# Expert rows transposed on their way in by DMA, as two planes of 16-bit halves, with the picks for four blocks taken together

## The reference, cut to what matters

```python
x = x + 0.5 * ffn(layernorm(x), ...)      # 32 experts, 6 per token, and shared experts
x = x + attn(layernorm(x), ...)           # local in segments of 64, global over 64 means
x = x + 0.5 * ffn(layernorm(x), ...)      # the same weights again
# in ffn, for every expert e that a token chose, with weight c:
g = xf @ gu[:128].T ; u = xf @ gu[128:].T
routed += c * (silu(g) * u @ dn.T)
```

## Time and profile before

| | us |
|---|---|
| median of three runs | 1511.45 (1508.77 to 1520.38) |
| profiled execution, its span | 1514.0 |
| first load of expert rows to last issue of answers, first expert stage (L515, L672) | 272.1 to about 630 |
| the same, second expert stage | 1049.9 to 1407.8 |
| PE busy | 1311.2 (87%) |
| DVE busy | 1092.3 (72%) |
| POOL busy | 921.6 (61%) |
| ACT busy | 745.8 (49%) |

### The profile page before, as it was taken

One profiled execution on the slowest core, in us unless ns is written; L12 is line 12 of the kernel. 1 busy time (PEld: TensorE's weight loads), 2 busy tenths in 40 slices (PEclk: granted clock), 3 DMA queues, 4 the chain that ended last, 5 costly groups with the idle time before them and its releaser, 6 DMA issues.

```text
span 1514.0 us, 50415 instructions
## 1 busy us (share of the span) xinstructions
PE 1311.2 (87%) x10768; PEld 1150.5 (76%) x10769; DVE 1092.3 (72%) x5484; ACT 745.8 (49%) x2296; POOL 921.6 (61%) x981
## 2 busy tenths in 40 slices
PE   6877772799999999789989998952999999999986
PEld 5766661699999999678766766742999999999765
DVE  6676654478888888576368888863788888888576
ACT  3433320466666666300356666721666666666100
POOL 3777777466666666422017776775566666666687
PEclk9776775899999999899699999955999999999998
DMA  9963333465556555397003333444565556564698
GB/s 316 404 248 130 126 130 127 146 184 184 186 185 190 181 187 178 119 330 256 1 29 136 142 131 131 147 174 144 176 188 187 184 183 186 180 184 139 231 315 280
DMA packets 155771, 275.35 MB, mean 182 GB/s; under 512 B 28966, under 2 KB 108091, under 8 KB 155712
## 3 DMA queue, kind: packets, MB, share of 16 engines
q1 hardware_dynamic: 115776, 161.32, 34.6%
q0 software_dynamic: 39936, 113.33, 20.2%
HBM read 147.64 MB, written 135.27 MB: 187 GB/s over the span
## 4 chain that ended last, share of the span: by engine, by line
PE 30%; DVE 7%; DMA 5%; issue 4%; POOL 3%; ACT 1%; DVEq 0%; SPq 0%; POOLq 0%; ACTq 0%
PE ps L711 26%; DMA ans<-answers 4%; PE ps L831 3%; POOL dispatch_rows L656 2%; DVE smax L1926 1%; DVE yb L1846 1%; POOL xres L693 1%; DVE stats L1469 0%; DVE prob L1936 0%; DVE rstd L1456 0%; DVE newt L1454 0%; DVE newt L1455 0%; PE ps L719 0%; DMA blk<-normed_transposed 0%; POOL answers L672 0%
## 5 line engine op out<-in xcount | busy, mean ns | idle before, releaser
L711 PE MATMUL ps<-xbt,ans 128*128 128x128 f32 x3584 | 477.0, 276 | 0.3 <-ACT ans L1274 0.3
L711 PEld LDWEIGHTS ps<-xbt,ans 128*128 128x128 f32 x3584 | 439.0, 193 | 0.9 <-ACT ans L1274 0.8
L672 POOL DMA_INDIRECT answers<-yb,didx x224 | 220.2, 983 | 160.9 <-issue 118.0
L672 POOL DMA_INDIRECT answers<-ans,didx x224 | 220.1, 983 | 122.2 <-issue 120.2
L1703 DVE SCALAR_TENSOR_TENSOR picked<-iota_e,etab,blk 128x32 f32<-128x32 f32 x896 | 190.7, 250 | 119.9 <-DVE yb L1724 40.1
L656 POOL DMA_INDIRECT dispatch_rows<-blk,idx x192 | 188.4, 981 | 142.9 <-issue 129.3
L1274 ACT COPY ans<-wgu 128x512 f32 x448 | 274.6, 613 | 0.2 <-issue 0.2
L711 PE MATMUL ps<-wdn,hb 128*128 x896 | 267.6, 381 | 1.3 <-DVE ans L1724 1.3
L632 POOL DMA_INDIRECT dispatch_rows<-blk,idx x192 | 187.3, 976 | 79.0 <-issue 57.2
L1280 ACT ACTIVATE sg<-ps 128x128 f32<-128x128 f32 x448 | 124.4, 278 | 218.5 <-PE ps L711 216.8
L831 PE MATMUL ps<-ident,blk 128*128 128x128 f32 x896 | 172.9, 275 | 33.6 <-DMA blk<-dispatch_rows 33.6
(11 more groups left out here) (230 smaller groups left out, 1996.7 us busy)
## 6 DMA issues: line engine op xcount, KB each, us to landing
blk<-dispatch_rows SPq DMA_DIRECT2D x448, 160.0 KB
ans<-answers SPq DMA_DIRECT2D x54, 512.0 KB, 4.9
ans<-answers SPq DMA_DIRECT2D x54, 256.0 KB, 4.8
wgu<-in_gate_up SPq DMA_DIRECT2D x32, 256.0 KB
dispatch_rows<-blk,idx POOLq DMA_INDIRECT x384, 2.5
dispatch_rows<-padt SPq DMA_DIRECT2D x32, 160.0 KB
yb<-answers SPq DMA_DIRECT2D x10, 512.0 KB, 4.8
wdn<-in_down SPq DMA_DIRECT2D x16, 256.0 KB
```

The lines of the kernel that those rows point to most:

```text
L672: pool.indirect_dma_start(out=answers_dram, out_offset=bass.IndirectOffsetOnAxis(ap=didx[:, q:q + 1], axis=0), in_=block_answers(q), in_of ...
L711: return nc.tensor.matmul(out_, lhs, rhs, start=start, stop=stop)
```

## The change: what it does

**The rows.** A row in `dispatch_rows` keeps its 1,280 bytes and is laid out as two planes of 640 bytes. Plane 0 holds 256 16-bit halves (the one half of each float) and the 32 weights. Plane 1 holds the other halves and the 32 destinations. ACT's copy in `act_route_rows` writes the planes: it moves 2 x 2 x 256 elements of 16 bits per partition in place of 512 floats. The scatters of the routing name the same bytes as 16-bit elements.

**The loads.** SP issues two DMAs per block in place of one. A transposing DMA takes 256 source rows (128 rows x 2 planes) of 256 16-bit elements and writes them transposed, so that the two halves of each float lie side by side again: 128 partitions x 2 x 128 floats. There are eight such buffers. A second DMA loads the weights and destinations, 2 runs of 128 bytes per row, into one of two buffers, each for four blocks. The register with the first row number is read one block ahead, by `reg_load`, without the range check.

**What goes.** PE's two transpositions per block, ACT's copy of them, and their semaphores go.

**The picks.** DVE compares the expert number for four blocks at once (`mark`), multiplies with the loaded pairs (`take`), reduces (`reduce_`) and makes four indices (`lists`), one of these per step: four instructions for four blocks in place of 20 records. PE's down product has four PSUM banks in place of two.

```diff
-COL_W, COL_DEST = D, D + E
+PLANE = ROW // 2
+COL_W, COL_DEST = D // 2, PLANE + D // 2
...
-        LOADS, ANSWERS = 4, 8
+        LOADS, ANSWERS, PICKED, LISTS = 8, 8, 4, 16
...
-            def body(g, peeled):
-                for q in range(LOADS):
-                    n = g * LOADS + q
-                    first = sp.value_load(itab[0:1, bass.ds(n + 2 * P, 1)], min_val=0, max_val=E * CAP - P)
-
-                    if not peeled:
-                        sp.wait_ge(s.tx, n - (LOADS - 1))
-                        sp.wait_ge(s.pick, n * 2 - (2 * LOADS - 2))
-                    sp.dma_start(block_rows(q), rows_dram[bass.ds(first, P), :]).then_inc(s.ld[q], 16)
...
+            def load(n, q, m=None):
+                at_ = sp.snap(first[q % 2], min_val=0, max_val=E * CAP - P)
+                if m is None or n + 1 < NB:
+                    sp.reg_load(first[1 - q % 2], itab[0:1, bass.ds(n + 1 + 2 * P, 1)])
+                block_rows = rows_dram[bass.ds(at_, P), :]
+
+                positive(sp, s.gu, n - (LOADS - 1))
+                sp.dma_start_transpose(
+                    out=turned_halves(q % LOADS),
+                    in_=block_rows.bitcast(U16).rearrange("r (h x) -> (r h) x", h=2)[:, 0:D]
+                    ).then_inc(s.ld[q % LOADS], 16)
+
+                positive(sp, s.pick, n // PICKED - 1 if isinstance(n, int) else turn_of(n, q) - 1)
+                sp.dma_start(pairs_of(q // PICKED % 2)[:, q % PICKED],
+                             block_rows.rearrange("r (h x) -> r h x", h=2)[:, :, D // 2:]
+                             ).then_inc(s.pairs[q // PICKED % 2], 16)
...
-            def tx(n, q):
-
-                b = q % LOADS
-                pe.wait_ge(s.ld[b], loaded(s, n, b))
-                for c in range(KC):
-                    m = pe.transpose(ps[:, TX + q % 2, c * P:(c + 1) * P], block_rows(b)[:, c * P:(c + 1) * P], ident[:])
-                m.then_inc(s.tx, 1)
...
-            act.copy(rows[:, 2 * k:2 * k + 2, 0:D], xn[:, 2 * k:2 * k + 2, :]).then_inc(s.rx, 1)
+            act.copy(planes(rows[:, 2 * k:2 * k + 2, :])[:, :, :, 0:D],
+                     halves(xn[:, 2 * k:2 * k + 2, :])).then_inc(s.rx, 1)
...
-            def xt_copy(n, j):
-                act.wait_ge(s.tx, n + 1)
-                positive(act, s.gu, n - 1)
-                act.copy(xbt[:, j, :], ps[:, TX + j, 0:D]).then_inc(s.xt, 1)
...
+            def mark(n):
+                st.did(v.tensor_tensor(
+                    mine, iota_e[:].unsqueeze(1).to_broadcast([P, PICKED, E]),
+                    etab[:, bass.ds(n, PICKED)].unsqueeze(2).to_broadcast([P, PICKED, E]), ALU.is_equal))
+
+            def take(k, paired):
+                v.wait_ge(s.pairs[k], paired)
+                st.sync()
+                v.tensor_tensor(picked, pairs_of(k), mine.unsqueeze(2).to_broadcast([P, PICKED, 2, E]),
+                                ALU.mult).then_inc(s.pick, 1)
+
+            def reduce_(k, group):
+                v.wait_ge(s.pick, group + 1)
+                st.did(v.tensor_reduce(wd[:, k], picked, X_AXIS, ALU.add))
+
+            def lists(n, q):
+                k = q // PICKED % 2
+                st.sync()
+                st.did(v.tensor_tensor(didx[:, q:q + PICKED], wd[:, k, :, 1], skip[:, bass.ds(n, PICKED)], ALU.add))
```

More of the change, by code:

```diff
@@ L197, in build, with planes, halves @@
         rows = blk
+        def planes(tiles):
+            return tiles.bitcast(U16).rearrange("p q (h x) -> p q h x", h=2)
+        def halves(tiles):
+            return tiles.bitcast(U16).rearrange("p q (d h) -> p q h d", h=2)
         xbt = sb("xbt", [P, 2, D])
@@ L349, in __init__ @@
                     self.sh_x = s("sh_x")
-        LOADS, ANSWERS = 4, 8
+        LOADS, ANSWERS, PICKED, LISTS = 8, 8, 4, 16
         row_loads = [sem(f"ex_ld{q}") for q in range(LOADS)]
+        pair_loads = [sem(f"ex_pairs{k}") for k in range(2)]
         class ExpertSems:
@@ L505, in sp_experts, with turn_of @@
             sp.wait_ge(ld_small, N_SMALL)
-            def body(g, peeled):
-                for q in range(LOADS):
-                    n = g * LOADS + q
-                    first = sp.value_load(itab[0:1, bass.ds(n + 2 * P, 1)], min_val=0, max_val=E * CAP - P)
-                    if not peeled:
-                        sp.wait_ge(s.tx, n - (LOADS - 1))
-                        sp.wait_ge(s.pick, n * 2 - (2 * LOADS - 2))
-                    sp.dma_start(block_rows(q), rows_dram[bass.ds(first, P), :]).then_inc(s.ld[q], 16)
-            body(0, True)
-            with sp.Fori(1, NB // LOADS) as g:
-                body(g, False)
+            first = [sp.alloc_register(f"first{k}_{s.n}") for k in range(2)]
+            def load(n, q, m=None):
[12 more added lines that the diff above has]
+                             ).then_inc(s.pairs[q // PICKED % 2], 16)
+            def turn_of(n, q):
+                return groups[0] * 2 + q // PICKED
+            groups = [None]
+            sp.reg_load(first[0], itab[0:1, 2 * P:2 * P + 1])
+            for n in range(8):
+                load(n, n, m=0)
+            with sp.Fori(1, NB // 8 - 1) as g:
+                groups[0] = g
+                for q in range(8):
+                    load(g * 8 + q, q)
+            for n in range(NB - 8, NB):
+                load(n, n % 8, m=0)
         def sp_sum(sp, x, s):
@@ L666, in pool_experts @@
         def pool_experts(pool, s):
-            with pool.Fori(0, NB // ANSWERS) as g:
-                for q in range(ANSWERS):
-                    pool.wait_ge(s.y, g * ANSWERS + (q + 1))
+            with pool.Fori(0, NB // LISTS) as g:
+                for q in range(LISTS):
+                    pool.wait_ge(s.y, g * LISTS + (q + 1))
                     pool.sem_inc(s.take, 1)
@@ L1722, in step @@
-                    v.wait_ge(s.d, n - 1)
-                    v.wait_ge(s.pick, n * 2 - 2)
-                    v.tensor_scalar(block_answers(k), ps[:, DN + j, 0:D], wcol[:, at_:at_ + 1], None, ALU.mult).then_inc(s.y, 1)
-                    st.sync()
-                if m is None or n + 2 < NB:
-                    pick(n + 2, (q + 2) % 8)
-            pick(0, 0)
-            pick(1, 1)
-            for n in range(16):
-                step(n, n % 8, m=0)
-            with v.Fori(2, NB // 8 - 1) as g:
-                for q in range(8):
-                    st.rebase(g * 8 + (start + q - 2))
-                    step(g * 8 + q, q)
@@ L1737, in v_experts @@
-            st.rebase(start + NB - 8 - 2)
-            for n in range(NB - 8, NB + 2):
-                step(n, n % 8, m=0)
+                             16 * ((n - 2) // ANSWERS) if isinstance(n, int) else turn * 32 + 16 * ((q - 2) // ANSWERS))
+                    st.sync()
+                    v.tensor_scalar(block_answers(k), ps[:, DN + b % 4, 0:D], wd[:, b // PICKED % 2, b % PICKED, 0:1],
+                                    None, ALU.mult).then_inc(s.y, 1)
+                phase, group = q % PICKED, q // PICKED + 1
@@ new lines, in v_experts @@
+            mark(0)
+            take(0, s.paired_by_now + 64)
+            reduce_(0, 0)
+            lists(0, 0)
+            for n in range(LISTS):
+                step(n, n, None, m=0)
+            base_n = st.base + st.n
+            with v.Fori(1, NB // LISTS - 1) as g:
+                st.rebase(g * 12 + (base_n - 12))
+                for q in range(LISTS):
+                    step(g * LISTS + q, q, g)
+                assert st.n == 12, st.n
+            st.rebase(base_n + (NB // LISTS - 2) * 12)
@@ L1741, in v_sum @@
+            for n in range(NB - LISTS, NB + 2):
+                step(n, n % LISTS, None, m=0)
         def v_sum(v, st, s):
```

90 lines of the change are left out of this document (45 added, 45 removed).

## The result

The changed kernel takes **2016.8 us** (four runs, 2011.8 to 2021.4) against 1510.9 (four runs) before: a ratio of 1.335 [1.331, 1.338]. Forecast was 1543 within 1440 to 1650. The direction was right; the rise was put at 32 us and is 506. In twelve of the eighteen runs of the experiments (the first three of pairs_on_act, all of before_no_turn, the first two of two_plain_runs, both of half_tiles, plain_load and every_other) the kernel before itself took 1895 to 1908 us, for a cause that stays open, so those are read by their ratio to it and by the middle values of SP's instructions; in the other six it took 1509 to 1511.

The account below looks back on a forecast made before the run. PE was taken to bound the kernel at 1.542 us a block, then SP's list at 0.910 + 0.365 + 0.333 = 1.608: 29.6 us over 448 blocks, plus 2 for ACT's copy, +32 us, forecast 1543 us, range 1440 to 1650.

Parts of the forecast that it names:

- The step that failed: In SP's new list, the transposing DMA's issue was taken as 333 ns, like the nearest row, a plain load.
- The pair load: SP's second DMA per block, for weights and destinations: its issue was put at 365 ns, bounds 333 and 496.
- The rest of SP's list: SP's work per block beside the two DMA issues: 492 ns of instructions, 58 of ALU operations, 360 of gaps, 0.91 us.
- SP at 86% of a block: Before the change, SP's instructions and gaps were summed to 1.33 of the 1.54 us block, which no busy row shows.
- ACT's row copy: In routing and attention: the copy grows from 0.62 to about 1.10 us; 2 us charged, bounds 0 and 15.
- DVE's `take`: In the expert stage: late pairs hold DVE once in four blocks, PE goes on two blocks without `hb`; nothing charged.
- The ends of a stage: From a stage's last load to its last answer, 14.0 us before: one landing of 2.25 us and eight steps, 12.5 us.
- DMA engines: Rival: short runs and the transposing stream fill the DMA engines, about 1.9 us a block, 1672 us; chance 0.17.
- PE's clock: Rival: PE at 76% busy gets a lower clock; one block in ten at 1.2 GHz adds 37 us; no chance of its own.
- The faster case: Rival: SP doesn't stand still for the table read, its list is 1.30 us beside POOL's 1.28; 1390 to 1496 us; chance 0.28.
- The signs named beforehand: Forecast wrong if SP's issues come over 1.65 or under 1.5 us apart, `hb` ends PE's idle, DMA share above 0.9, clock below 1.00.

Follow-up runs that it names:

- pairs_on_act: The changed kernel with the pair loads issued by ACT instead of SP: 1661.6 us, ratio 1.100; three earlier runs 1901.4 to 1917.3 us, ratios near 1.00 to 1.010.
- before_no_turn: The kernel before without PE's transpositions and ACT's copy of them, multiplying untransposed rows: 1845.0, 1859.3 and 1852.5 us, the last two at ratios 0.972 and 0.976.
- two_plain_runs: The changed kernel with two plain one-run loads per block, rows as floats, untransposed, ACT's old row copy: 1546.9 us, ratio 1.024; earlier ratios 1.010 and 1.017.
- half_tiles: The changed kernel with half of each transposing DMA left out, 128 of 256 source columns loaded: 2205.6 and 2206.3 us, the second with a ratio of 1.154.
- plain_load: The changed kernel with a plain two-run DMA of the same bytes, untransposed, in place of the transposing one: 2087.9 us beside 1903.3 for the kernel before.
- every_other: The changed kernel with the transposing DMA issued only for every second block, the odd block multiplying the even one's rows: 1959.6 us, ratio 1.033.

## Why the prediction was wrong, point by point

- **The step that failed** is "The issue of a transposing DMA is in no row. Bounds are 0 from below, and 496 ns from above. I take 333". It is 1208 ns, 0.875 more, and worth 448 x 0.875 = 392 us, four fifths of the miss. The upper bound was drawn from plain DMAs, which are another kind of instruction; nothing in the trace limited the unknown one to their range. Even at 496 ns the sum gives 1.771 us a block and 1616 us, inside the range of 1440 to 1650, so nothing in the range stood for a dearer issue.
- **The pair load**, put at 365 ns within 333 to 496, is 558: 448 x 0.193 = 86 us. A two-run load of the earlier trace rows cost 396 at its least, but the two-run loads of these kernels cost 543 (plain_load) to 558. The 735 ns at the upper end of the same row was a warning not used.
- **The rest of SP's list** was nearly right: 0.910 us forecast by instruction sums and 40-ns gaps, 0.863 measured. In part that is luck: a MOVE with its gap (69 ns) was counted that does not come, while the turn of the loop (44 ns a block) was left out and the table read put 27 ns too low. With the right prices the same sum gives 0.910 + 0.558 + 1.208 = 2.676 us a block, and 1511 + 448 x 1.134 + 2 = 2021 us, against 2017. So the mechanism stood and two terms of it did not. The same omission of the loop's turn put SP at 86% of a block before, where its waits make it about 92%.
- **ACT's row copy**: the duration was right (1.10 forecast, 1.046 measured), the 2 us were not. The 7 us of copy in attention and a lower clock go with 6.7 to 12.8 us more between the stages, inside the bound of 15.
- **DVE's `take`**: charging nothing was right for the time, since SP decides, but the sign given was wrong. I said PE's idle time would be ended by the transposed rows' landing, and that an idle time ended by `hb` would mean a late `take` and a wrong forecast. It was `hb` (364.6 us), and the late `take` was SP's list.
- **The ends of a stage** were forecast to go from 14.0 to 12.5 us and went to 17.0 and 15.8: the wrong way, and small, 5 us for both stages.
- **DMA engines** (1672, 17%): no. The share fell from 0.60 to 0.46; per block 0.46 x 2.63 = 1.21 us in place of 0.93. Short runs do cost, but far from the 1.77 and 2.6 us that I worked out from 70 ns a row. The Trainium skill, page "Advanced Engine Details and Errata", section "X-Bar Transpose (TRN2)", says transposing DMAs are as fast as regular ones. For the transfer the trace is near it: 2.7 us from the start of the issue to the landing, by the middle value, against 2.25 for the plain load of the earlier trace rows, and the longer issue is part of the 2.7. For the issue it is not: 1208 against 333 ns.
- **The page "DMA: Bandwidth & Descriptors"** of the Trainium skill, section "Why a DMA increments its semaphore by 16 and not by 1", with its 631 and 512 cycles, gave a ratio of 1.23. Measured here is 1208/333 = 3.6, and 3.3 for the smallest of the three sizes. The measurement decides.
- **PE's clock** fell to 0.83 in the expert stages as the rival said it could, but SP's list sets the block there whatever the clock. PE was waiting, up to 5.0 us at a stretch between 320 and 580, and with the pairs on ACT, at 1.85 us a block, it read 1.00 again.
- **The faster case** needed the table read to be free for SP. It was not (278 ns, and the list came out as summed), and it would have needed a cheap transposing issue too.
- **The signs named beforehand** did their work: issues more than 1.65 us apart (2.63), PE's idle time ended by `hb`, and a clock below 1.00 all came. Only the first names the cause; the other two follow from it.

## What to carry to other kernels

When an edit puts a DMA kind on a queue that the trace has never shown there, the rows of other kinds set no upper bound on its issue time: work out at which price the queue becomes the bound (here 0.27 us, with the rest at 0.910 + 0.365) and let that decide the range. Sum the list of the issuing queue instruction by instruction, with the turn of the loop, since no busy share shows it; confirm it by the mean spacing over a whole stage, and look for waits in the gaps and in the view of waits, not in the durations. Where all engines look half idle and one waits on a load that lands quickly once issued, look at when it was issued.

## What the runs showed of the hardware that was not expected

- A transposing DMA of 16-bit elements holds its queue for 1.1 to 1.2 us, nearly whatever its size: 1110 ns for 128 x 128, 1117 for 256 x 128, 1208 for 256 x 256. A plain DMA of 128 rows of one run each holds it for 333 ns, with runs of 256 bytes as with 1,024 and 1,280.
- SP's wait for a buffer shows as a gap between two instructions and not in the duration of any (kernel before: 53.7 us of waits, no operation on L514 over 56 ns).
- A plain DMA of two runs per row holds its queue for 543 to 558 ns, on SP (558) as on ACT (551).
- ACT copies 1,024 16-bit elements per partition in 1046 ns with a contiguous destination and in 1338 ns with both sides strided, against 620 for the same bytes as 512 floats.
- Of the kernels here that compute the whole result none is faster than the kernel before; the nearest with the change in it is pairs_on_act, 1661.6 us. Without the transposition, before_no_turn is faster (0.97 to 0.98 of the kernel before) and two_plain_runs is not (1546.9 us).
